# GpSimd's gathers in a graph network's message stage: which engine's signal opens a group of rows

## The reference

```
# layer 0, for every edge e with source s and target d
y   = silu(silu(radial @ W1 + b1) @ W2 + b2)       # 8 -> 64 -> 64
tpw = y @ W3 + b3                                   # 256 weights, four 8x8 blocks
m0  = a*(einsum(hs[s]*sh0, W00) + c*einsum(hv[s]*sh1, W110))
m1  = a*(einsum(hs[s], sh1, W01) + einsum(hv[s]*sh0, W10))
agg = segment_sum([m0, m1], d) / 4
x   = layernorm(x + self(x) + agg)
# layer 1
e     = leaky_relu(s_src[s] + s_dst[d]);  alpha = softmax of e over the edges of a target
x     = layernorm(x + segment_sum(x[s] * alpha, d))
```

## Time and profile before

| | |
|---|---|
| time, median of 3 runs (lowest to highest) | 9807.54 us (9800.2 to 9808.86) |
| the profiled execution's own time | 9820.55 us |
| its span, first to last instruction | 9818.8 us |
| mean granted TensorE clock | 0.62 |
| busy: PE, DVE, ACT, POOL | 30%, 43%, 20%, 69% of the span |
| DMA | 31 GB/s over the span |

### The profile page before, as it was taken

The page is one execution under the profiler, slowest core; times in us unless marked ns, Lnnn a source line. Parts: engine busy times, 40 slices in busy tenths (PEclk is TensorE's granted clock), DMA queues, the critical chain, the costliest instruction groups (busy, mean ns, idle before and its releaser), DMA issues.

```text
span 9818.8 us, 46930 instructions
## 1 busy us (share of the span) xinstructions
PE 2922.1 (30%) x8550; PEld 1835.1 (19%) x8550; DVE 4243.2 (43%) x7138; ACT 1924.5 (20%) x3182; POOL 6768.2 (69%) x6664
## 2 busy tenths in 40 slices
PE   5555555555655556566530000000000000000000
PEld 3333333333333333333320000000000000000000
DVE  6767767677777767777732111111111111111112
ACT  2333333233333333222200000010000010100000
POOL 5666666666666666666657777777777777777776
PEclk7777777777777777777755555555555555555555
DMA  2111111111111111111111111111111111111111
GB/s 79 34 36 35 36 35 34 37 34 36 35 34 37 34 37 34 31 29 31 31 23 22 27 25 25 25 25 25 25 25 25 25 25 25 25 25 25 25 25 23
DMA packets 320586, 300.13 MB, mean 31 GB/s; under 512 B 173460, under 2 KB 276999, under 8 KB 319903
## 3 DMA queue, kind: packets, MB, share of 16 engines
q0 software_dynamic: 216352, 159.92, 11.7%
q1 hardware_dynamic: 104220, 140.09, 4.2%
HBM read 188.98 MB, written 110.53 MB: 31 GB/s over the span
## 4 chain that ended last, share of the span: by engine, by line
POOL 37%; issue 24%; another core or an unknown queue 15%; DVE 14%; PE 4%; ACT 3%; DMA 2%; DVEq 0%; SPq 0%; POOLq 0%; ACTq 0%
POOL prod L317 33%; DVE red L677 3%; POOL rows L317 3%; DVE prod L663 3%; DVE red L675 2%; DVE prod L658 2%; PE tpw L415 1%; POOL starts L321 1%; PE hid L404 1%; ACT hid L467 1%; DVE red L689 1%; DMA rows<-in_x_wide,idx 1%; PE hid L408 1%; ACT hid L461 1%
## 5 line engine op out<-in xcount | busy, mean ns | idle before, releaser
L317 POOL DMA_INDIRECT rows<-in_x_wide,idx x3126 | 3093.3, 990 | 1708.0 <-issue 921.2
L317 POOL DMA_INDIRECT prod<-table,idx x3125 | 3276.4, 1048 | 1079.8 <-issue 1079.8
L415 PE MATMUL tpw<-w3s,hid 128*128 128x256 f32 x6252 | 1845.0, 456 | 58.0 <-issue 36.1
L870 DVE TENSOR_TENSOR score<-prod,big 128x25 f32<-128x25 f32 x125 | 26.2, 209 | 3668.4 <-DMA prod<-table,idx 3668.4
L415 PEld LDWEIGHTS tpw<-w3s,hid 128*128 128x128 f32 x6252 | 1387.7, 229 | 655.9 <-issue 361.4
L436 PE MATMUL hid<-ident,ends 128*33 128x128 f32 x2 | 0.6, 420 | 4350.1 <-DVEq L921 4350.1
L658 DVE TENSOR_TENSOR prod<-tpw,rows 128x1152 f32<-128x1152 f32 x521 | 698.0, 1340 | 1221.8 <-remote 1188.5
L467 ACT ACTIVATE hid<-hid,b2s 64x384 f32<-64x384 f32 x1044 | 601.7, 576 | 2792.1 <-remote 1795.4
L408 PE MATMUL hid<-hid,w2s 128*128 128x384 f32 x1044 | 560.7, 625 | 1944.6 <-ACT hid L461 1649.2
L436 PEld LDWEIGHTS hid<-ident,ends 128*33 128x33 f32 x2 | 0.2, 146 | 4350.2 <-DVEq L921 4350.2
L675 DVE TENSOR_REDUCE red<-prod 128x144 f32<-128x1152 f32 x521 | 702.7, 1349 | 4.5
(11 more groups left out here) (142 smaller groups left out, 2275.2 us busy)
## 6 DMA issues: line engine op xcount, KB each, us to landing
scan<-prod SPq DMA_DIRECT2D x125, 425.0 KB
rows<-in_x_wide,idx POOLq DMA_INDIRECT x3126
prod<-table,idx POOLq DMA_INDIRECT x3125
scan<-sums SPq DMA_DIRECT2D x130, 384.0 KB
rad<-in_radial_t SPq DMA_DIRECT2D x262, 48.0 KB
big<-in_sh SPq DMA_DIRECT2D x1, 6288.0 KB
idx<-in_src SPq DMA_DIRECT2D x262, 6.0 KB
msgs<-scan,end_i POOLq DMA_INDIRECT x200
```

Of the source, the lines that this page charges most:

```text
L317: return pool.indirect_dma_start(out=dest, out_offset=None, in_=source, in_offset=bass.IndirectOffsetOnAxis(ap=index, axis=0))
L415: mm = pe.matmul(tpw_v(b)[:, t, :], hid2[:, b, at:at + P], w3s[:, :], start=True, stop=True)
```

## The change

One line differs, the wait at the head of a group in `gather_again`. POOL now waits for `tpw_ready` >= G-1: the end of TensorE's `layer3` of group G-2. Since `layer3` of group G-2 itself begins only after `products` of group G-4 (L412), the slot is still free when POOL writes it.

```
             def gather_again(it, k):
-                pool.wait_ge(tpw_used, it * SLOTS + k - 1)
+                pool.wait_ge(tpw_ready, it * SLOTS + k - 1)
                 if k % HALF == 0:
                     pool.wait_ge(idx_in[k // HALF], it * 16 + 16)
                 pool.nop(nofuse=True)
```

## The result

| | before | after |
|---|---|---|
| time, median of 4 runs (lowest to highest) | 9808.2 us (9800.2 to 9808.86) | 10134.45 us (10098.62 to 10152.72) |
| ratio | | 1.033 (95%: 1.030 to 1.036) |
| profiled execution | 9820.55 us | 10098.62 us |

The change made the kernel 3.3% slower. I had said 9640 us.

What follows compares the result with a forecast made beforehand. POOL's run plus one stop bounds the message stage, 37.8 us an iteration; 31.9 + 4.6 = 36.5 us, 1.3 less, times 130.2 iterations saves 169 us: 9640 us forecast, range 9260 to 10000.

Steps and rivals of the forecast that it cites:

- What bounds the kernel: Message stage: an iteration of 37.8 us is POOL's 31.9 us run plus one 5.9 us stop, ended by TensorE's held signals.
- Step 1: Direct delay at POOL's k0 head: it now needs k2's `layer3`, so it would stand 7.9 us later.
- Step 2: New stop at POOL's k2 head, waiting for a held TensorE signal: 3.5 us a stop against 5.9 now.
- the pattern: TensorE's signals are held late in a long POOL run and come about 2.5 us after POOL's last gather.
- Step 3: POOL's stops at four heads an iteration: between one and two, taken as 1.3, costing 4.6 us.
- Step 4: Later rows, `hv`, `products`, `layer3`, resume: a loop of 15.4 to 18.0 us against POOL's 17.4; costs 0 to 0.6, counted nothing.
- The first: Rival: TensorE's signals are late for its own reasons, so 7.9 us an iteration is added: 10840 us; 4 in 100.
- The second: Rival: POOL's stops multiply to two or three an iteration, 9950 or 10410 us; 25 in 100, mostly at two.

Runs made afterwards that it cites:

- k123_again: Kernel before, with TensorE's signal waited for at the k1, k2 and k3 heads only and VectorE's use of the rows at k0: ratio 1.0013.
- b_half: Kernel before, with each gather fetching the rows of 64 edges of 128 from the second iteration on: ratio 0.9922.
- a_radearly: Changed kernel, with SyncE fetching slots 0 and 1's radial inputs before storing the sums, and each radial fetch before its half's index fetch: 9639.46 us, ratio 0.9727.
- after_again: The changed kernel, unaltered, run again in another set on another chip: ratio 1.0395.
- b_radearly: Kernel before, with SyncE fetching radial inputs ahead of the store of the sums and of each half's index fetch: ratio 0.9992.

## Why the prediction was wrong

**What bounds the kernel** was right: POOL's run of 31.9 us plus one stop, and held signals at the end of the stop. Where no signal is held the kernel before has 8508 to 8554 us, and in its variants there POOL's stops of 5.9 us are gone (k123_again: 44.1 us of POOL waits for L415). In b_half, whose heads all wait for VectorE as in the kernel before, POOL's waits for L663 are 44.8 us in all, none over 0.3 us. That also bears out the reading of rows 3, that the stop is the hold and not VectorE's own time.

**Step 1** gave the right dependence, the k0 head on `layer3` of k2, and then the wrong weight. I let it count once, as a shift, and put the stop at the k2 head. It is the k0 head that stops: 123 of 151 stops, 977.6 of 1035.4 us by my count.

**Step 2 is the one that failed.** It said that "by the pattern the signal comes 2.5 us after its last gather" and priced a stop at 3.5 us. That is the price of a signal whose work is done. With VectorE no longer between POOL and TensorE, POOL comes to the k0 head before TensorE has started the work: 2.34 us to L415's start, 4.97 us of L415, 0.87 to resume, less 0.3, is 7.9 us against the 7.80 measured. TensorE's lateness was made of the radial fetch, in SyncE's order behind the store and, by the packets, 7.1 us behind it where 1.7 us are enough without held signals. a_radearly shows it by taking it away: the stop becomes 4.26 us, and the ratio 0.973. In its place stands then a stop of about the price that step 2 gave, at another head.

**Step 3** had 1.3 stops an iteration; 151 of over 0.3 us in 129 iterations are 1.2. That count was right, and of no use with the wrong price.

**Step 4** found the loop and mis-sized it. Its terms against the iteration of after_again: pair landed and prepared 9.0, measured 8.93 (1777.45 to 1786.38); `products` 2.6, measured 2.61; `layer3` 2.9 or 5.5, measured 4.97; resume 0.9, measured 0.88. Missing were 2.02 us, in which TensorE gets through L404, late behind ScalarE's sums. And POOL's work beside it was put at 17.4 us; there it is 16.6 (1777.45 to 1794.06). So the loop is 19.4 and not 15.4 to 18.0 us, its cost 2.8 and not 0 to 0.6 us. "A stop covers it" was wrong too: the loop is the stop. This alone, without any hold, is 335 us (after_again). The earlier trace rows had shown ScalarE's L467 11.76 us idle and TensorE cold behind it; I read both as held signals only, and not as the next loop.

**The rivals.** The first had the right mechanism in kind, TensorE late for its own reasons, with a price that was too high: I let the 7.9 us come on top of the old stop of 5.9 us, while they replace it (7.80 for 5.85, times 123 and 103). I gave it 4 in 100. The second (more stops) had the nearest time, 9950, and the wrong mechanism. By the Trainium skill's rule (Perfetto Trace Analysis, "Tensor Engine Instruction") that the prediction weighed, a signal follows real work; the trace after the change agrees, with 120 of 121 stops ending within 1.1 us of L415's recorded end.

**What I had asked the profile to show.** POOL's waits do name L415, VectorE's waits for "remote" vanished, and L640 stands idle 1673 us, 12.9 us an iteration, where I had 5 to 8; 1085.5 us of it name `hv`, for 587.6 us the profile names no releaser. POOL's busy time stayed. "Step 2 is wrong if a stopped POOL waits over 4.1 us" is what happened.

**Left open.** What holds TensorE's signals and delays SyncE's transfers on some chips and not on others, and whether the two are one effect. Whether four instructions more or five fewer on SyncE move the time under held signals, and whether half the gathered rows would release them: the runs meant for it met the other kind.

## What to carry to other kernels

Before a wait is moved to an earlier producer, follow that producer's own queue back through every engine, DMA issues included: the old consumer may have been hiding how late it runs. A wait that a row shows as small (51 us for the radial inputs) tells only that something else was later still. Add up the new closed loop from row to row, with each engine's work that stands in line between, and with the clock that TensorE has after idling; and when a change is worth a few per cent, compare only inside a set of runs that share the kernel before. Where a record of an issue matters, look at the packets too: here they moved ahead of it.

## What the runs showed of the hardware

- The kernel before took 9906 us in one set and 8508 to 8554 us in four, each set on another chip: 16% apart, with the same instructions and nearly the same mean granted clock (0.62 and 0.63 to 0.64). Two things differ in the traces of the variants. In the message stage the one chip shows waits for "remote" (1176 us of VectorE's in b_radearly, 441 us of POOL's in a_radearly) and SyncE instructions over 0.6 us (786 of 1866 in a_radearly between 500 and 4000 us), the others none of either (0 of 1938 in after_again). And in the stages behind it the one is some 490 us longer (4862 against 4371 us, b_radearly and k123_again), its softmax gathers taking 1.05 us in place of 0.95.
- From the store's first packet to the radial fetch's it took 7.1 us (median) in the profile of the changed kernel and 1.7 us in after_again, the same program. SyncE's own records have 9.42 and 1.41 us; in the first profile the packets start ahead of the recorded issue in 82 of 174 radial fetches, in the second never.
- After TensorE had idled some 12 us, the 12 instructions of L415 took 4.97 us in place of 2.86, and L408 and L404 1.65 and 1.64 us in place of 0.81 and 0.91. In the loop above the two that nothing else covers, L415 and L404, make that some 2.8 us of 34 (an estimate from these rows).
